# Three target arrays, paired down products and longer rings in a routed feed-forward layer

## The reference

```python
scores = softmax(x @ gate_w.T)                       # 64 experts
topk_w, topk_idx = top_k(scores, 6)                  # six experts per token, weights normalised
g = einsum('ecd,efd->ecf', buf, w_gate)              # buf: the rows routed to each expert
u = einsum('ecd,efd->ecf', buf, w_up)                # F = 176
eo = einsum('ecf,edf->ecd', silu(g) * u, w_down)
y = zeros_like(x).at[st].add(eo[...] * weight)       # each row is added to its token
x = x + y + (silu(x @ sh_gate.T) * (x @ sh_up.T)) @ sh_down.T + ...   # shared expert, F = 352
```

## Time and profile before

| what | value |
|---|---|
| median of 3 runs | 542.45 us (541.57 to 545.41) |
| profiled execution, span from the first to the last instruction | 581.2 us |
| PE busy | 528.9 us, 91% of the span |
| VectorE / ScalarE / GpSimd busy | 348.5 / 301.3 / 334.4 us |
| mean granted TensorE clock | 0.941 |
| moved by DMA | 119.01 MB, mean 205 GB/s |

### The profile page before, as it was taken

One profiled execution on the slowest core, in us unless ns is written; L12 is line 12 of the kernel. 1 busy time (PEld: TensorE's weight loads), 2 busy tenths in 40 slices (PEclk: granted clock), 3 DMA queues, 4 the chain that ended last, 5 costly groups with the idle time before them and its releaser, 6 DMA issues.

```text
span 581.2 us, 13626 instructions
## 1 busy us (share of the span) xinstructions
PE 528.9 (91%) x4267; PEld 446.2 (77%) x4267; DVE 348.5 (60%) x1107; ACT 301.3 (52%) x899; POOL 334.4 (58%) x365
## 2 busy tenths in 40 slices
PE   8799998988989894969999999999988999999991
PEld 7698988888889883858877878787766787778681
DVE  4968877777777874756554555555454555455512
ACT  3797777778777863311234444455544444445410
POOL 4482254555444546575146766766666676678840
PEclk9898998889777976899999999999999999999997
DMA  9999997722222222122999999999989999977556
GB/s 292 388 373 394 404 390 280 228 84 84 73 74 74 83 74 88 57 98 78 321 267 300 252 245 230 236 244 251 251 217 231 241 238 233 231 143 115 73 116 140
DMA packets 65857, 119.01 MB, mean 205 GB/s; under 512 B 11216, under 2 KB 43280, under 8 KB 62704
## 3 DMA queue, kind: packets, MB, share of 16 engines
q0 software_dynamic: 24576, 56.39, 37.0%
q1 hardware_dynamic: 39584, 58.75, 33.2%
q10 hardware_dynamic: 1616, 2.90, 1.4%
HBM read 57.28 MB, written 60.23 MB: 202 GB/s over the span
## 4 chain that ended last, share of the span: by engine, by line
PE 75%; DVE 7%; issue 4%; another core or an unknown queue 4%; ACT 4%; POOL 2%; DMA 1%; ACTq 0%; DVEq 0%
PE PS L958 17%; PE PS L976 9%; PE PS L962 7%; PE PS L979 7%; PE PS L629 4%; PE PS L945 4%; PE PS L696 4%; PE PS L809 3%; PE PS L767 3%; PE PS L609 3%; PE PS L784 2%; PE PS L713 2%; PE PS L795 2%; PE PS L719 2%
## 5 line engine op out<-in xcount | busy, mean ns | idle before, releaser
L1836 POOL DMA_INDIRECT expert_rows<-XR,slot x96 | 95.1, 990 | 86.9 <-PE PS L629 58.7
L1859 POOL DMA_INDIRECT out<-YE,dest x64 | 93.6, 1462 | 45.2 <-issue 24.7
L1859 POOL DMA_INDIRECT acc_b<-YE,dest x64 | 93.7, 1465 | 37.4 <-issue 14.0
L1234 ACT ACTIVATE YE<-PS,wsel 104x256 f32<-104x256 f32 (+14 forms) x128 | 53.4, 467 | 96.5 <-PE PS L979 78.1
L1061 ACT ACTIVATE SMX<-SMX,smax 128x112 f32<-128x112 f32 x256 | 75.0, 392 | 0.2 <-DVE smax L1464 0.2
L1649 DVE TENSOR_TENSOR HE<-SL,PS 128x216 f32<-128x216 f32 (+12 forms) x64 | 23.2, 362 | 52.0 <-ACT SL L1221 39.5
L1070 ACT COPY PT<-PS 112x512 f32<-112x512 f32 x64 | 36.0, 595 | 21.0 <-remote 15.8
L767 PE MATMUL PS<-VW,PT 112*64 112x17 f32 x960 | 35.8, 213 | 11.2 <-issue 11.2
L1640 DVE COPY XET<-PS 128x432 f32<-128x432 f32 (+12 forms) x64 | 36.5, 572 | 15.6 <-PE PS L945 11.4
L1626 DVE SCALAR_TENSOR_TENSOR hit<-XG,by_rank 112x12 f32<-112x12 f32 (+3 forms) x64 | 14.6, 229 | 49.3 <-DMA out<-YE,dest 33.7
L767 PEld LDWEIGHTS PS<-VW,PT 112*64 112x64 f32 x960 | 32.6, 140 | 14.8 <-issue 12.7
(11 more groups left out here) (236 smaller groups left out, 1146.0 us busy)
## 6 DMA issues: line engine op xcount, KB each, us to landing
expert_rows<-zero POOLq DMA_DIRECT2D x24, 1088.0 KB, 14.0
W<-in_w SPq DMA_DIRECT2D x24, 368.0 KB
XG<-expert_rows SPq DMA_DIRECT2D x24, 238.0 KB
XB<-in_w SPq DMA_DIRECT2D x15, 368.0 KB
SMX<-in_w SPq DMA_DIRECT2D x15, 368.0 KB
XG<-expert_rows SPq DMA_DIRECT2D x24, 204.0 KB
W<-in_w SPq DMA_DIRECT2D x24, 128.0 KB
XG<-expert_rows SPq DMA_DIRECT2D x10, 272.0 KB
```

The costliest lines, as they stand in the source:

```text
L1234: act.mul(YE[0:h, e.slot, t, :], PS[0:h, 5 + t, e.odd * D:(e.odd + 1) * D], wsel[0:h, e.slot, t:t + 1]).then_inc(y_ready, 1)
L1836: pool.indirect_dma_start(rows, bass.IndirectOffsetOnAxis(ap=slot[:, d2 % UN, k:k + 1], axis=0), XR[:, d2 % UN, :], None, bounds_check=EX ...
L1859: pool.indirect_dma_start(target, bass.IndirectOffsetOnAxis(ap=dest[0:h, e.slot, t:t + 1], axis=0), YE[0:h, e.slot, t, :], None, bounds_ch ...
```

## The change

- Adds go into three arrays in turn, `acc_b`, `out` and the new `acc_c`; from expert 54 on into `acc_b` and `out` in turn. Expert e waits for the last expert of the same array. All three start as zeros, written by ScalarE's queue in steps 7 to 9 of the attention phase; the fills of `out` with X1 are gone.
- After expert 53 `acc_c` is loaded back (into XB), after the last adds `acc_b` (into SMX) and `out` (into XB), in quarters of four blocks; VectorE adds each to X1, and X1 is stored in quarters. The fold in memory is gone.
- `YE` has six slots, `dest` and `wsel` twelve, `HE` four (in the space of PT).
- PE works two experts ahead in `hidden` and four in `rows_t`, and does the down products of two experts at once after the odd one: both 128-row parts, then both 48-row parts. ScalarE and VectorE follow this order.
- SyncE loads the weights of p + 10 behind the rows of p + 4, once the down product of p - 2 is done.

The branch for crowded experts, which does not run here, is changed alike and left out.

```diff
+YS = 6
+LAST_C = 53
...
+    acc_c = nc.dram_tensor("acc_c", (T, D), F32, kind="Internal").ap()
...
-        XA = SMX[:, 0:NTL * D].rearrange("p (t d) -> p t d", t=NTL)
+        XA = SMX[:, :].rearrange("p (t d) -> p t d", t=NT)
...
-        wsel = sb("wsel", [P, UN, 2])
+        wsel = sb("wsel", [P, AHEAD, 2])
...
-        HE = sb("HE", [P, 2, 2, MAIN])
-        YE = sb("YE", [P, UN, 2, D])
+        HE = PT[:, :, :, :].rearrange("p g j q -> p (g j q)").rearrange("p (u t n) -> p u t n", u=UN, t=2)
+        YE = sb("YE", [P, YS, 2, D])
...
+        def target(e):
+
+            return e.off % 3 if e.i is not None or e.off <= LAST_C else e.off % 2
...
+        def y_home(e):
+
+            return e.off % YS
...
                     expert_rows(expert(n), n % UN, 0, 2, HALF[n])
                     if p < 2:
                         weights(expert(AHEAD - 2 + p), AHEAD - 2 + p)
-                    if p + AHEAD < EX:
-                        sp.wait_ge(dn_done, p + 1)
-                        weights(expert(p + AHEAD), p % AHEAD)
+                    elif p - 2 + AHEAD < EX:
+                        sp.wait_ge(dn_done, p - 1)
+                        weights(expert(p - 2 + AHEAD), (p - 2) % AHEAD)
...
+            last = Step(LAST_C)
+            sp.wait_ge(y_stored[y_home(last)], last.turn(32, 32, YS))
+            sp.wait_ge(dn_done, LAST_C + 2)
+            sp.dma_start(XB[:, :, :], tokens(acc_c, 0, NT)).then_inc(c_back, 16)
+            sp.wait_ge(b_closed, 1)
+            for k in range(4):
+                sp.dma_start(XA[:, k * NQ:(k + 1) * NQ, :], tokens(acc_b, k * NQ, NQ)).then_inc(b_back[k], 16)
+            sp.wait_ge(out_closed, 1)
+            sp.wait_ge(summed, 4)
+            for k in range(4):
+                sp.dma_start(XB[:, k * NQ:(k + 1) * NQ, :], tokens(out, k * NQ, NQ)).then_inc(out_back[k], 16)
+            for k in range(4):
+                sp.wait_ge(summed, 9 + k)
+                sp.dma_start(tokens(out, k * NQ, NQ), X1[:, k * NQ:(k + 1) * NQ, :]).then_inc(out_stored, 16)
...
+                def down_two(e):
+
+                    pe.wait_ge(h_ready, e.times(2, 4))
+                    pe.wait_ge(w2_doubled, e.times(1, 2))
                     if not e.first():
                         pe.wait_ge(y_ready, sums_before(e, nt))
...
+                    down_head(e, True)
+                    down_head(e + 1, False)
+                    down_tail(e, False)
+                    down_tail(e + 1, True)
...
+                def step(e):
+                    if has(e + 2, end):
+                        hidden(e + 2)
+                    if has(e + 4, end):
+                        rows_t(e + 4)
+                    if e.odd:
+                        down_two(e - 1)
...
                 hidden(Step(0))
+                rows_t(Step(2))
                 pe.wait_ge(sh_add, NT - NTL)
+                hidden(Step(1))
+                rows_t(Step(3))
                 in_flight(pe, step, half is even_half)
...
-                if s == LF + 1:
+                if s in (LF + 1, LF + 2, LF + 3):
...
+                    sums = (acc_b, out, acc_c)[s - LF - 1]
...
+                def step(e):
+                    if has(e + 2, end):
+                        silus(e + 2)
                         doubled(e + 2)
+                    if e.odd:
+                        weighted(e - 1)
+                        weighted(e)
...
-                    if not e.first(UN):
-                        dve.wait_ge(y_stored[j], adds_before(e, nt))
...
+                    elif not e.first(AHEAD):
+                        dve.wait_ge(y_stored[y_home(e)], e.turn(32, -32, YS))
...
                 dve.wait_ge(d2_done, NPAIR)
+                dve.wait_ge(c_back, 16)
+                for k in range(4):
+                    add_quarter(k, XB, 1 + k)
                 tail_product(NPAIR)
+                for k in range(4):
+                    dve.wait_ge(b_back[k], 16)
+                    add_quarter(k, XA, 5 + k)
                 tail_product(NPAIR + 1)
...
+                for k in range(3):
+                    dve.wait_ge(out_back[k], 16)
+                    add_quarter(k, XB, 9 + k)
                 pair_add(NPAIR)
                 pair_add(NPAIR + 1)
+                dve.wait_ge(sh_add, NT)
+                dve.wait_ge(out_back[3], 16)
+                add_quarter(3, XB, 12)
...
+                pool.memset(YE[:, UN:YS, :, :], 0.0)
...
-            pool.wait_ge(x1_ready, NT)
-            fill(NT - NTL, NTL)
-            pool.wait_ge(sh_add, 2 * NQ)
-            fill(0, 2 * NQ)
...
-                if not e.first(2):
-                    before = e - 2
-                    hold(pool, y_stored[before.slot], before.turn(32, 32))
-                elif e.odd:
-                    pool.wait_ge(out_filled, 16 * 3)
-                added(e, out if e.odd else acc_b, 2, h)
+                if not e.first(3):
+                    before = same_target(e)
+                    hold(pool, y_stored[y_home(before)], before.turn(32, 32, YS))
+                added(e, (acc_b, out, acc_c)[target(e)], 2, h)
...
-            pool.sem_inc(adds_closed, 1)
-            fold()
-            pool.wait_ge(folded, 16)
+            pool.sem_inc(out_closed, 1)
```

More of the change, by code:

```diff
@@ L1246, in step @@
                     weighted(e)
-                    if nt == 2 and has(e + 2, end):
+                def step(e):
+                    if has(e + 2, end):
+                        silus(e + 2)
                         doubled(e + 2)
+                    if e.odd:
+                        weighted(e - 1)
+                        weighted(e)
                 if nt == 1:
                     silus(Step(EX))
-                    rest_in_flight(act, step)
+                    rest_in_flight(act, step_one)
                     return
@@ L1645, in product @@
                     dve.wait_ge(silu_ready, e.times(2, 1))
-                    if not e.first(2):
-                        dve.wait_ge(dn_done, e.times(1, -1))
-                    dve.tensor_tensor(HE[:, q, 0, 0:n], SL[:, q, 0, 0:n], PS[:, 2 + q, MAIN:MAIN + n], ALU.mult)\
+                    if not e.first(UN):
+                        dve.wait_ge(dn_done, e.times(1, 1 - UN))
+                    dve.tensor_tensor(HE[:, e.slot, 0, 0:n], SL[:, q, 0, 0:n], PS[:, 2 + q, MAIN:MAIN + n], ALU.mult)\
                        .then_inc(h_ready, 1)
@@ L1656, in tail_products, with ahead @@
                         c = slice(t * h, (t + 1) * h)
-                        i = dve.tensor_tensor(HE[64 * t:64 * t + FT, q, 1, c], SL[0:FT, q, 1, c],
+                        i = dve.tensor_tensor(HE[64 * t:64 * t + FT, e.slot, 1, c], SL[0:FT, q, 1, c],
                                               PS[64:64 + FT, TAIL[q], c], ALU.mult)
                     i.then_inc(h_ready, 1)
-                def step(e):
-                    if has(e + 1, end):
-                        product(e + 1)
-                    if has(e + 2, end):
-                        rows_t(e + 2)
-                    if has(e + 1, end):
-                        tail_products(e + 1)
-                        choices(e + 1)
+                lead = nt
+                def ahead(e):
+                    if has(e, end):
+                        product(e)
+                    if has(e + lead, end):
+                        rows_t(e + lead)
+                    if has(e, end):
+                        tail_products(e)
+                        choices(e)
+                def step(e):
+                    ahead(e + nt)
                 first = Step(0 if nt == 2 else EX)
@@ L1677, in experts @@
                 product(first)
-                tail_products(first)
                 if nt == 1:
+                    tail_products(first)
                     rest_in_flight(dve, step)
                 else:
+                    rows_t(first + 2)
+                    tail_products(first)
+                    ahead(first + 1)
                     in_flight(dve, step, half is even_half)
@@ L1881, in rest @@
                 before = e - 1
-                hold(pool, y_stored[before.slot], before.turn(16, 16 * EX // UN + 16))
+                hold(pool, y_stored[y_home(before)], before.turn(16, 16 * y_uses(y_home(before)) + 16, YS))
                 added(e, acc_b, 1, P)
-            pool.wait_ge(sh_add, 3 * NQ)
-            fill(2 * NQ, NQ)
-            pool.wait_ge(b_ready, 16)
+            pool.wait_ge(sums_ready, 16 * 3)
             def landed(nt):
-                for j in range(UN):
-                    pool.wait_ge(y_stored[j], 16 * nt * EX // UN)
-            def fold():
-                def piece(v):
-                    return v[0:(NT - NTL) * P, :].rearrange("(p n) d -> p (n d)", p=P).rearrange("p (k w) -> p k w", w=4 * D)
-                pool.dma_start(piece(out), piece(acc_b), accum_op=ALU.add, max_dma_last_dim=4096).then_inc(folded, 16)
+                for j in range(YS):
+                    uses = y_uses(j) if nt == 2 else y_uses(j, 2 * EX)
```

(1 more changed line is left out.)

140 lines of the change are left out of this document (78 added, 62 removed).

## The result

The changed kernel takes 594.71 us (median of 4 runs, 592.27 to 601.06). The kernel before took 543.93 us beside it (4 runs, 541.57 to 545.53). The ratio is 1.095, with a 95% interval of 1.088 to 1.103: slower, inside the forecast range of 539 to 600, and 19 us above the forecast 576. The profiled execution has a span of 590.5 us and a time of 592.27.

The account below looks back on a forecast made before the run. PE's pace was taken to bound the expert phase. The profile's 581.2 us plus 37.5 for the experts less 2.8 at the end gave 615.9; the added 34.7 on the median gave 576 us, range 539 to 600.

Parts of the forecast that it names:

- The loop: Expert pairs: odd rows queue on SyncE behind the previous pair's down product and three weight DMAs; 9.54 us instead of 8.29.
- L: Time from issue to landing of an odd expert's row load on SyncE's queue; taken as 3.7 us, range 3.2 to 4.0.
- rows that pass them: Row loads overtaking their weights in SyncE's queue: L would be 3.4 and the time about 568 us.
- the floor with nothing ahead: Lower bound of L for a row load with an empty queue: 2.1 us, the smallest landing in the trace.
- The rival in which the rows come in time: Expert pairs: no stall if L is 2.05, so PE's savings show; 525 us, chance 0.12.
- The start: First experts: expert 4's row load issued as before, expert 5's rows landing at 303.0, first pair's first tail ending at 305.9.
- The expert phase: First hidden product to last tail product: PE's last tail ends at 590.1 against 552.67, 37.5 us later.
- The end: After the last tail product: four adds, landing, loads and stores take 25.6 us instead of 28.5, 2.8 us less.
- GpSimd as a bound: Adds among the experts: no case of its own, as 3.44 us per expert is under the loop's 4.77.
- just late: Expert pairs: rows come slightly late at L = 2.1, a pair takes 7.94 us; 539 us, chance 0.10.
- the clock rival: PE standing in every pair loses its clock for a fifth of the phase, 21 us more; 597 us, chance 0.08.

Follow-up runs that it names:

- sp_delay: The changed kernel with two more reads of the expert's number on SyncE before each of 26 odd experts' row loads; 611.64 us, one run.
- singles: The changed kernel with down products one by one and the lookahead of the kernel before on all engines; 545.12 us, 1.007 of the kernel before.
- before_again: The kernel before, unchanged, profiled once more; 545.61 us in one run, span 543.8 us.
- ring6_two: ring6 with the sums and closing part of the kernel before (two arrays, fills, fold); 545.66 us, 1.004 of the kernel before.
- ring6: The changed kernel with six slots of rows instead of four, SyncE loading rows of p + 6 instead of p + 4; 538.96 us, 0.993 of the kernel before.

## Why the prediction was right, and where it was wrong

**The loop was right, step by step.** For the 26 pairs, in the mean and by the starts of PE's weight loads: from a pair's first tail product to the issue of the row load (0.68 + 2.98 = 3.66 us in the prediction) 3.88; from issue to the transposes (L = 3.7) 3.39; transposes and head products up to the tail (0.36 + 1.82 = 2.18) 2.40. Together 9.67 where 9.54 was said. That PE would wait 26 times was right (25 times for an odd expert's rows, once for an even one's), and so was that pairs go back to 7.5 us when weights run out (7.56, 7.56, 7.54).

**L was put a little too high.** The last packet came 2.89 us after the issue in the mean (2.38 to 4.06), and PE began 0.5 us later. Both DMA rates in the earlier trace rows were those of full queues; in the loop the queues have slack (0.87). With the rows 1.1 us further behind the weights it was 2.47. In the views of issues and landings, 269 to 520 us of the kernel after (KB, median us to landing):

```profile
XG<-expert_rows SPq DMA_DIRECT2D x24, 238.0 KB, 3.9
```

That row has loads of odd and of even experts together.

The Trainium skill (DMA: Bandwidth & Descriptors, Queues, rings and completion order) has descriptors consumed in ring order, by which I had put L at 4.0. The packets of SyncE's queue, told apart by their sizes, agree with that order: in the kernel after 92% of an odd load's packets start behind the last packet of the three weight transfers ahead of it, in sp_delay all of them. So the rows did go behind their weights, though the measured 3.39 is close to the 3.4 that I gave to rows that pass them; the price of 4.0 was too high.

Where I took 2.1 us, the landing of a 1 KB load, as the floor with nothing ahead, sp_delay shows that floor for a row load: its weights' packets have all started before the first row packet, which starts 0.95 to 1.39 us after the issue, and the last still comes at 2.47. So only some 0.4 us of the 2.89 is the weights' share, by the difference. The rival in which the rows come in time needed an L of 2.05; the shortest of the 26 was 2.78.

**The start was over-estimated.** The first pair's first tail starts 14.8 us after the first hidden product (253.51 to 268.27) and ends some 15.4 after it, where 18.5 was said. The step that failed is taking the row load of expert 4 over unchanged: 295.96 - 287.39 = 8.57 us after the first hidden product. In the kernel after, SyncE's queue has it at 258.99, 5.5 after, and that of expert 5 at 262.74, 9.2 after, where 11.9 was said. The order in front of expert 4's load is the same in both kernels, the weights of experts 4 to 9; but from the first row load to that of expert 4 SyncE took 17.2 us (241.84 to 258.99) where it had taken 19.6 (276.35 to 295.96). In singles it took 17.4, so that comes without the pairs; why isn't shown.

**The expert phase came out within 1.4 us** (301.3 against 302.7), by errors of opposite sign, which is luck in the sum: the start 3.1 us too long, the pairs 0.13 x 26 = 3.4 too short, and the last ten experts 1.7 too long. Against a phase of 261.3 in before_again it adds 40.0 us, where I had 37.5, since the profile I read from was 4 us long there.

**The end had the wrong sign.** I said 25.6 us in place of 28.5; it took 35.7. Three terms were too small. Four adds behind the last tail were really the end of nine without a longer pause (551.99 to 568.23): the last two pairs come within 6.70 and 4.71 us, and four adds take 6.9, so GpSimd was behind: 13.5 us where 4 x 1.72 = 6.9 was said. The landing took 4.3 (568.23 to 572.54) where the smallest landing, 2.1, was taken; acc_b's load was moving at the time, and whether that is the reason isn't shown. Loads, adds and stores took 18.0 (572.54 to 590.5) for 16.6. That is 6.6 + 2.2 + 1.4 = 10.2, the whole error. The end of singles, 4.7 us longer with the old order, shows that more than half of the 8.4 us over before_again comes with the design; the rest I put down to GpSimd's queue behind the pairs, which no run separates.

**The third array was undervalued.** I gave the rings and the array up to 5.6 us of PE's waiting and dismissed GpSimd as a bound. In the old order they gave 2. But ring6_two shows that pairs at PE's own pace need the third array: without it GpSimd falls behind and bounds the last pairs and the end, which I had ruled out.

**The rivals.** Rows in time and just late were refuted by the 26 waits. The clock did fall here and there, which I had named as a sign of being wrong: in four stretches among the experts (382.10 to 385.50, 419.65 to 423.05, 429.90 to 433.25, 440.15 to 443.50) the granted clock is 0.50, the lower level of 1.2 GHz, each time 0.3 to 1.4 us after a stand of PE had ended. The stretches around two of them, cut a little beside these bounds, so that 0.63 and 0.52 are means over both levels:

```profile
425.00:429.00 4.00, 2.10 (x18) 1.86 (x16) 2.28 (x9) 1.90 (x7) 3.39 (x3) 1.00 0.87 211
429.00:432.40 3.40, 3.39 (x14) 1.85 (x14) 1.64 (x7) 0.00 (x0) 2.17 (x2) 0.63 0.97 249
432.40:439.50 7.10, 5.08 (x37) 4.14 (x36) 2.57 (x9) 3.40 (x10) 3.60 (x3) 0.94 0.70 154
440.00:443.50 3.50, 3.50 (x12) 2.01 (x10) 1.76 (x7) 0.00 (x0) 1.58 (x2) 0.52 1.01 244
```

In the four pairs it hit, the time from transposes to tail was 2.95 to 3.92 us in place of 2.24, 4.3 us in all. The rival had 21. That one stand in the stretch from 256 us had left the clock at 1.00 spoke for a single stand, and here 22 of 26 left it there as well; it did not speak for all. The Trainium skill (TensorE: Matmul & The Clock Gate, The HAM clock gate) has activity release the throttle. The traces agree: in ring6, where PE doesn't stand among the pairs, the granted clock is 1.00 throughout them.

**Sum.** Phase +40.0, end +8.4, start of the experts -1.7: 46.7 us between the spans of after and before_again, and 50.8 between the medians. The forecast had +34.7: against the 46.7 its end is short by 11.2, its phase by 2.5 (the base 4.0 long, the phase after 1.4 too long), and it had nothing for the start, -1.7. The other 4 us stand between spans and medians: the profiled execution was the fastest of its four, 2.4 us under their median, and before_again lay 1.7 above that of the kernel before. The longer executions of the kernel after show a lower mean granted clock, 0.956 and 0.954 at 592 us, 0.946 at 597 and 0.943 at 601. That fits more stretches at the lower level, so the clock rival may weigh more in the median than in the profile; where those executions lost it isn't shown.

## What to carry to other kernels

When an engine is made to look further ahead, check that every ring it reads from grows by as much: four slots read four ahead left no room to load early here, and any wait in the loading queue then sits in the loop from one step to the next. Walk that loop from release to release before counting what the reorder saves; here 0.38 us a pair was bought with 2.00. A queue that only keeps pace (GpSimd's adds, 6.9 us of a 7.67 us pair) should be looked at where the steps get shorter, at the end above all, since there its backlog is the time.

## What the runs showed of the hardware

- A mean DMA share of 0.99 was no bound here: the same transfers ran at 257 GB/s in ring6 where the earlier trace rows shows 242.
- GpSimd's issues of indirect adds took 1.43 us, but 1.57 to 2.22 while VectorE ran its adds of 128 x 1024 floats: 1.57 at 551.99 and 2.21 at 553.87 in the kernel after, beside VectorE's four from 551.03 to 556.03, and 2.05 at 494.23 and 2.22 at 496.58 in ring6, beside those from 493.74 to 498.74. The small operations of the experts show no such effect.
- An accumulating transfer beside a load of 2 MB seems to land late: in ring6 the next add into out behind the one at 479.62 began only at 487.28, after the load issued at 477.39. That it waited for that landing follows from the code's order; no row names it.
- A row load of 170 to 272 KB with no packet of SyncE's queue left to start in front of it (sp_delay) had its first packet 0.95 to 1.39 us after the issue and its last at 2.47 in the mean; behind three weight transfers (the kernel after) the last came at 2.89.
